# Attention and clustered feed-forward layer on one core: the last quad's threshold by token, TensorE taking any over tokens, two dense tiles moved out of unit 31

## The reference, cut to what matters

```python
x = x + attention(layernorm(x), w_qkv, w_o)     # 32 heads, 8 kv heads, causal, sqrt-distance bias
y = layernorm(x)
dots = softmax(y @ centroids.T / 0.1)           # 64 clusters
hits = dots > 0.01
query_sel = any(hits, axis=clusters)            # one flag per token
cluster_sel = any(hits, axis=tokens)            # one flag per cluster, over all 2048 tokens
row_sel = cluster_sel[assignments]              # one flag per output column
dense = y @ weight.T + bias
x = x + where(query_sel & row_sel, dense, 0)
```

## Time and profile before

| what | us |
|---|---|
| runs: 1267.18, 1268.92, 1269.65; median | 1268.92 |
| the profiled execution's own time | 1267.08 |
| its span, first to last instruction | 1265.4 |
| TensorE busy | 1242.9 (98%) |
| TensorE weight loads | 1050.6 (83%) |
| VectorE busy | 767.6 (61%) |
| ScalarE busy | 751.8 (59%) |
| GpSimd busy | 515.5 (41%) |

### The profile page before, as it was taken

One profiled execution on the slowest core, in us unless ns is written; L12 is line 12 of the kernel. 1 busy time (PEld: TensorE's weight loads), 2 busy tenths in 40 slices (PEclk: granted clock), 3 DMA queues, 4 the chain that ended last, 5 costly groups with the idle time before them and its releaser, 6 DMA issues.

```text
span 1265.4 us, 21888 instructions
## 1 busy us (share of the span) xinstructions
PE 1242.9 (98%) x6166; PEld 1050.6 (83%) x6166; DVE 767.6 (61%) x2160; ACT 751.8 (59%) x2154; POOL 515.5 (41%) x476
## 2 busy tenths in 40 slices
PE   7899999999999999999999999999999999999997
PEld 6688888888888888888888888888888888888876
DVE  8777555555555555565555555655555556667677
ACT  3776566666655666666556666665565666656543
POOL 5322645227342455226442364327362364223223
PEclk9999999999999999999999999999999999999999
DMA  6422334334332343424333344323343343412103
GB/s 195 161 87 88 117 124 157 108 108 141 94 132 89 120 145 124 133 99 133 102 123 107 119 147 124 125 91 128 99 146 116 111 146 116 134 62 99 49 21 133
DMA packets 162377, 147.14 MB, mean 116 GB/s; under 512 B 10032, under 2 KB 123696, under 8 KB 162352
## 3 DMA queue, kind: packets, MB, share of 16 engines
q1 hardware_dynamic: 156528, 128.48, 30.6%
q0 software_dynamic: 5824, 18.36, 4.9%
HBM read 84.67 MB, written 62.13 MB: 116 GB/s over the span
## 4 chain that ended last, share of the span: by engine, by line
PE 87%; DVE 6%; ACT 3%; issue 2%; DMA 1%; POOL 0%; DVEq 0%; SPq 0%; ACTq 0%
PE ps L1206 81%; PE ps L1285 3%; PE ps L1286 1%; ACT prob L678 1%; ACT prob L669 1%; DVE ring_whole L905 1%; DVE stats L826 1%; PE ps L1226 1%; DVE qT_lo L880 1%; DVE rs L851 0%; DVE prob L865 0%; DVE prob L942 0%; DMA acc<-in_L_attn_hidden_states 0%; DVE acc L1127 0%; DVE selected L984 0%
## 5 line engine op out<-in xcount | busy, mean ns | idle before, releaser
L1206 PE MATMUL ps<-xnT,wqkv_hi 128*128 (+1 forms) x1568 | 486.4, 391 | 5.0 <-DVE negmax L942 2.8
L515 POOL TENSOR_TENSOR ring<-ring_whole,pT_hi 128x512 fp32r<-128x512 f32 x189 | 243.7, 1289 | 486.6 <-ACT pT_hi L658 486.3
L1206 PEld LDWEIGHTS ps<-xnT,wqkv_hi 128*128 128x128 f32 x1568 | 292.1, 188 | 66.6 <-issue 5.0
L669 ACT ACTIVATE prob<-prob,negmax 128x128 f32<-128x128 f32 (+1 forms) x512 | 226.8, 445 | 181.9 <-DVE negmax L942 180.9
L1206 PE MATMUL ps<-xnT,wqkv_lo 128*128 (+1 forms) x784 | 305.8, 390 | 0.0
L678 ACT ACTIVATE prob<-prob,rinv 128x128 f32<-128x128 f32 (+1 forms) x512 | 190.3, 445 | 62.5 <-DVE rinv L950 62.5
L1206 PE MATMUL ps<-wo_hi,oT_hi 128*128 128x512 f32 x512 | 201.8, 394 | 0.0
L1206 PE MATMUL ps<-wo_lo,oT_hi 128*128 128x512 f32 x512 | 199.8, 390 | 0.0
L1206 PE MATMUL ps<-wo_hi,oT_lo 128*128 128x512 f32 x512 | 199.3, 389 | 0.0
L1206 PEld LDWEIGHTS ps<-xnT,wqkv_lo 128*128 128x128 f32 x784 | 147.4, 188 | 31.1
L922 DVE TENSOR_TENSOR acc<-ps,acc 128x512 f32 (+1 forms) x128 | 88.5, 691 | 128.1 <-PE ps L1206 127.9
(11 more groups left out here) (125 smaller groups left out, 1717.2 us busy)
## 6 DMA issues: line engine op xcount, KB each, us to landing
turned<-ring_whole SPq DMA_DIRECT2D x189, 256.0 KB, 2.1
ring_whole<-turned SPq DMA_DIRECT2D x189, 256.0 KB, 3.0
turned_v<-vT SPq DMA_DIRECT2D x32, 256.0 KB, 2.0
vT<-turned_v SPq DMA_DIRECT2D x31, 256.0 KB, 2.8
raw<-in_L_attn_w_qkv POOLq DMA_DIRECT2D x28, 256.0 KB, 3.2
raw<-in_L_attn_w_o POOLq DMA_DIRECT2D x28, 256.0 KB, 3.5
raw<-in_L_attn_w_qkv POOLq DMA_DIRECT2D x28, 128.0 KB, 3.5
acc<-in_L_attn_hidden_states SPq DMA_DIRECT2D x3, 1024.0 KB, 8.2
```

Source lines behind the costliest of these rows:

```text
L515: pool.tensor_tensor(ring_slot(c), whole_slot(c), pT_hi[:, c % 2, :].bitcast(F32), ALU.subtract).then_inc(pT_lo_done, 1)
L669: ins = act.activation(s, s, ACT.Exp, bias=negmax[:, n:n + 1], scale=-1.0, accum_out=rowsum[:, n:n + 1])
L1206: ins = pe.matmul(dst, l, r, start=start and m == 0, stop=stop and m == n - 1)
```

## The change

- Quad 1's `dense(1,0)` and `dense(1,1)`, with their `dense_part`, leave unit 31 and head the tail. On VectorE `dense_part(1,0)` stands between `invert_sums` 2 and 3, and `dense_part(1,1)` behind 3. In the tail `apply_v(32, 0)` moves ahead of `dense(1,3)`.
- Quad 3's logits are computed with tokens on the partitions at once (`logits_by_token`): per tile four matmuls of 128 columns (hi part of x with both halves of `cT`) and four of 64 (lo part of x with the hi half), each with its own stationary operand. ScalarE copies the lo half to SBUF (`copy_low`), VectorE adds it onto the hi half in PSUM and takes the maximum (`last_max`), ScalarE writes the exponentials over the logits in PSUM (`last_exps`), and VectorE compares them with sum times threshold in one instruction (`last_cluster_hits`).
- The maximum over quads and tiles (`any_hit`, quad 3's `quad_hits`) is gone: seven small matmuls accumulate the hits of three quads and of quad 3's four tiles.
- The waits for the mask move ahead of `dense(2,2,(2,3))`; the first half of `dense(2,0)` is put before `transpose_logits(2)`, the second half behind it. VectorE does `cluster_bias(2)` before `ln_lo(7)`, `finish(0,4)` directly behind `cluster_sel`, and both `dense_part(2,0)` and `(2,1)` behind that. ScalarE does `scaled_bias(2)` behind the last exponentials.

```diff
...
@@ -339,6 +343,10 @@
         def whole_slot(c):
 
             return ring_whole[:, c % RING, :]
+
+        def last_logits():
+
+            return ps[:, LAST_LOGITS, :].rearrange("p (t s c) -> p t s c", t=TPQ, s=2)
 
         def by_tail(u, c):
 
@@ -694,6 +702,19 @@
                     at = slice(j * CLUSTERS, (j + 1) * CLUSTERS)
                     ins = act.activation(cl_exp[:, at], ps[:, logit_bank(p), at], ACT.Exp,
                                          bias=cl_bias[:, j:j + 1], scale=INV_TEMP, accum_out=cl_sum[:, j:j + 1])
+                ins.then_inc(cl_exp_done, 1)
+
+            def copy_low():
+
+                act.wait_ge(logit_mm, QUADS)
+                act.activation(logitT[:, 0:TPQ * CLUSTERS].rearrange("p (t c) -> p t c", t=TPQ), last_logits()[:, :, 1, :],
+                               ACT.Copy).then_inc(low_copied, 1)
+
+            def last_exps():
+                act.wait_ge(cl_max_done, QUADS)
+                for j in range(TPQ):
+                    e = last_logits()[:, j, 0, :]
+                    ins = act.activation(e, e, ACT.Exp, bias=cl_bias[:, j:j + 1], scale=INV_TEMP, accum_out=cl_sum[:, j:j + 1])
                 ins.then_inc(cl_exp_done, 1)
 
             def scaled_bias(p):
@@ -803,9 +824,9 @@
             for j in range(TPQ):
                 ln_hi(7, j, LAST)
             cluster_exps(2)
-            copy_logits(3)
+            copy_low()
+            last_exps()
             scaled_bias(2)
-            cluster_exps(3)
             scaled_bias(3)
 
 
@@ -974,6 +995,31 @@
                 dve.tensor_reduce(quad_hits[:, bass.ds(p * CLUSTERS, CLUSTERS)],
                                   cl_exp[:].rearrange("p (t c) -> p c t", c=CLUSTERS), AX_X, ALU.max).then_inc(ffn_step, 1)
                 ffn_wait(p, 4)
+                dve.sem_inc(hits_done, 1)
+
+            def last_max():
+
+                dve.wait_ge(low_copied, 1)
+                logits = last_logits()[:, :, 0, :]
+                dve.tensor_tensor(logits, logits, logitT[:, 0:TPQ * CLUSTERS].rearrange("p (t c) -> p t c", t=TPQ),
+                                  ALU.add).then_inc(last_step, 1)
+                dve.wait_ge(last_step, 1)
+                dve.tensor_reduce(cl_nmax[:], logits, AX_X, ALU.max, negate=True).then_inc(last_step, 1)
+                dve.wait_ge(last_step, 2)
+                dve.tensor_scalar(cl_bias[:], cl_nmax[:], INV_TEMP, None, ALU.mult).then_inc(cl_max_done, 1)
+
+            def last_cluster_hits():
+
+                dve.wait_ge(cl_exp_done, QUADS + 1)
+                dve.tensor_scalar(cl_rinv[:], cl_sum[:], THRESHOLD, None, ALU.mult).then_inc(last_step, 1)
+                dve.wait_ge(last_step, 3)
+                hits = last_hits[:].rearrange("p (t c) -> p t c", t=TPQ)
+                dve.tensor_tensor(hits, last_logits()[:, :, 0, :],
+                                  cl_rinv[:].rearrange("p (t a) -> p t a", a=1).broadcast_to([P, TPQ, CLUSTERS]),
+                                  ALU.is_gt).then_inc(last_ready, 1)
+                dve.wait_ge(last_ready, 1)
+                dve.tensor_reduce(selects(QUADS - 1), hits, AX_X, ALU.max).then_inc(last_step, 1)
+                dve.wait_ge(last_step, 4)
                 dve.sem_inc(hits_done, 1)
 
             def dense_part(p, quad, j):
@@ -1037,6 +1083,7 @@
                 if p is not None:
                     cluster_bias(p)
                     cluster_hits(p)
+                if p == 0:
                     dense_part(p, source, 0)
                 if proj:
                     add_bias(u, 2)
@@ -1045,7 +1092,7 @@
                     add_bias(u, 3)
                     if not is_first(u):
                         invert_sums(u, 0)
-                if p is not None:
+                if p == 0:
                     dense_part(p, source, 1)
                 if attn:
                     add_out(u, 2)
@@ -1128,7 +1175,9 @@
                                     selected[:, at].rearrange("p (t n) -> p t n", t=n)).then_inc(final, n)
 
             invert_sums(u - 1, 2)
+            dense_part(1, 1, 0)
             invert_sums(u - 1, 3)
+            dense_part(1, 1, 1)
             oT_lo_part(u, 0)
             tail_pT_lo_part(3)
             dve.wait_ge(added, u * QTILES)
@@ -1164,24 +1213,21 @@
             ln_scale(7)
             for j in range(TPQ):
                 ln_apply(7, j, 3)
+            cluster_bias(2)
             for j in range(TPQ):
                 ln_lo(7, j, LAST)
-            cluster_bias(2)
             cluster_hits(2)
-            cluster_bias(3)
-            dense_part(2, 2, 0)
-            cluster_hits(3)
-
-            dve.tensor_reduce(any_hit[:], quad_hits[:].rearrange("p (q c) -> p c q", c=CLUSTERS), AX_X,
-                              ALU.max).then_inc(any_ready, 1)
+            last_max()
+            last_cluster_hits()
             dve.wait_ge(sel_mm, 1)
             dve.tensor_scalar(cluster_sel[:], ps[0:CLUSTERS, PV[0], 0:P], 0.0, None, ALU.is_gt).then_inc(csel_ready, 1)
-            dense_part(2, 2, 1)
             dve.wait_ge(sel_mm, 2)
             finish(0, 4)
+            dense_part(2, 2, 0)
+            dense_part(2, 2, 1)
+            finish(4, 4)
             dense_part(2, 2, 2)
             dense_part(2, 2, 3)
-            finish(4, 4)
             dense_part(3, 3, 0)
             dve.wait_ge(dense_out, TPQ * QUADS)
             finish(8, 4)
@@ -1296,6 +1342,18 @@
                     for n, x in enumerate(ffn_x(p)):
                         ins = pe.matmul(ps[:, logit_bank(p), :], cT[:, c, :, :], x[:, c, :], start=c == n == 0, stop=c == NC - 1 and n == 1)
                 ins.then_inc(logitT_mm, 1)
+
+            def logits_by_token(p):
+
+                x_hi, x_lo = ffn_x(p)
+                for j in range(TPQ):
+                    pe.wait_ge(ln_lo_done, p * TPQ + TPQ * QUADS + j + 1)
+                    at = slice(j * P, (j + 1) * P)
+                    dst = ps[:, logit_bank(p), at]
+                    for c in range(NC):
+                        pe.matmul(dst, x_hi[:, c, at], cT[:, c, :, :], start=c == 0, stop=False)
+                        ins = pe.matmul(dst[:, 0:CLUSTERS], x_lo[:, c, at], cT[:, c, 0, :], start=False, stop=c == NC - 1)
+                ins.then_inc(logit_mm, 1)
 
             def transpose_logits(p):
                 pe.wait_ge(logitT_copied, p + 1)
@@ -1426,12 +1485,15 @@
 
             u = UNITS
             pe.wait_ge(v_lo_done, u)
+            pe.wait_ge(oT_lo_done, u * QTILES)
+            dense(1, 0)
+            dense(1, 1)
             pe.wait_ge(added, u * QTILES - 1)
             dense(1, 2)
+            pe.wait_ge(dense_out, TPQ + FFN_TAIL)
+            apply_v(u, 0)
             pe.wait_ge(scores_biased, u * SCORE_BANKS)
             dense(1, 3)
-            pe.wait_ge(dense_out, TPQ + FFN_TAIL)
-            apply_v(u, 0)
             pe.wait_ge(cl_exp_done, 3)
             transpose_probs(u, 3)
             apply_v(u, 1)
@@ -1458,27 +1520,31 @@
             project_out(u, 3)
             cluster_logits(2, u)
             pe.wait_ge(added, u * QTILES + 2)
-            dense(2, 0)
+            dense(2, 0, (0, 1))
             transpose_logits(2)
+            dense(2, 0, (2, 3))
             pe.wait_ge(added, u * QTILES + QTILES)
             for j in range(TPQ):
                 ln_transpose(7, j)
+            logits_by_token(3)
             dense(2, 1)
-            cluster_logits(3, None)
             dense(2, 2, (0, 1))
-            transpose_logits(3)
-            dense(2, 2, (2, 3))
-            pe.wait_ge(cl_exp_done, 4)
-            dense(2, 3)
-            dense(3, 0, (0,))
-            pe.wait_ge(any_ready, 1)
-
-            pe.matmul(ps[0:CLUSTERS, PV[0], 0:P], any_hit[:], ones[:], start=True, stop=True).then_inc(sel_mm, 1)
+            pe.wait_ge(hits_done, QUADS - 1)
+            any_hits = ps[0:CLUSTERS, PV[0], 0:P]
+            for p in range(QUADS - 1):
+                pe.matmul(any_hits, quad_hits[:, p * CLUSTERS:(p + 1) * CLUSTERS], ones[:], start=p == 0, stop=False)
+            pe.wait_ge(last_ready, 1)
+            for j in range(TPQ):
+                ins = pe.matmul(any_hits, last_hits[:, j * CLUSTERS:(j + 1) * CLUSTERS], ones[:], start=False, stop=j == TPQ - 1)
+            ins.then_inc(sel_mm, 1)
             pe.wait_ge(csel_ready, 1)
             pe.wait_ge(onehot_ready, 1)
 
             pe.matmul(ps[:, MASK_BANK, :], cluster_sel[:], onehot[:], start=True, stop=True).then_inc(sel_mm, 1)
-            dense(3, 0, (1, 2, 3))
+            dense(2, 2, (2, 3))
+            pe.wait_ge(cl_exp_done, QUADS)
+            dense(2, 3)
+            dense(3, 0)
             dense(3, 1)
             dense(3, 2)
             dense(3, 3)
```

## The result

The changed kernel's median is 1264.09 us (6 runs, 1262.71 to 1264.34), the kernel before has 1268.87 (6 runs): ratio 0.9966, 95% interval 0.9956 to 0.9976. In a second session, on one chip beside the first experiments, it was 1264.38 against 1267.46, ratio 0.9971 (0.996 to 0.9983). Faster, by 0.3%. The profiled execution took 1262.71, the fastest of its six.

The account below looks back on a forecast made before the run. TensorE and VectorE were both taken to press on the end, their last stretch starting from the mask. TensorE's -2.5 and VectorE's -0.45, against a schedule's 3.4, became -3.2: 1265.7 us from median 1268.92, range 1263.4 to 1268.8.

Parts of the forecast that it names:

- The sum: TensorE's terms to the end: -0.9 + 1.2 - 1.3 - 1.5 = -2.5 us, with VectorE adding -0.45.
- Two tiles leave unit 31: Unit 31 and tail start: 2.9 us of waits go, 2.25 come; output projection 0 starts 0.7 to 1.1 earlier, taken -0.9.
- Logits by token: Quad 3's logits on TensorE: 32 small matmuls at 0.11 take 3.5 us, plus 0.3 waiting; net +1.2 us.
- The threshold chain at the old forms' prices: Quad 3's threshold, table load to last compare (1234.0 to 1241.6), priced by old forms; its 2.8 us sum bounded by half and double.
- The hole: TensorE's gap in dense work at the mask: 1.9 us instead of 3.2, giving -1.3.
- The clock: TensorE behind the mask: the 2.4 GHz level holds throughout after the shorter hole, giving -1.5 us.
- The schedule's 3.4: Gain by the schedule at VectorE's end: last dense part and copy finish at 1259.4 against 1262.84, 3.4 us.
- The rounding up from 2.95 to 3.2: Final gain taken as -3.2 us, above the summed terms and 0.2 short of the schedule for semaphores.
- the moved tiles return nothing: Rival: unit 31's new waits equal the old ones; gain -2.3, 1266.6 us; chance 0.09.
- the clock still falls: Rival: TensorE's clock falls behind the 1.9 us hole, paying 1.5 again; gain -1.7, 1267.2 us; chance 0.16.
- small matmuls were not dear: Rival denied here: logits matmuls cost 0.21 to 0.227 each, ending 3.2 to 3.7 later; -0.5, 1268.4 us; chance 0.12.
- the queue was not held: Rival denied here: late threshold chain holds TensorE's queue; at double price, hole 4.7, +1.1, 1270.0 us; chance 0.07.

Follow-up runs that it names:

- the first experiments: Kernel before with moved tiles alone (1266.74 us); changed kernel with those tiles back (1265.68); kernel before with an unused SBUF tensor (1266.96); changed kernel again (1264.38).
- e5: Kernel before plus 18 unused transposes filling TensorE's hole before the any-hit matmul; 1268.30 us, ratio 1.0.
- e1: Kernel before with only dense(1,0) and dense(1,1) moved out of unit 31; 1266.74 us, ratio 0.9989.
- e3: Kernel before with one unused SBUF tensor declared, shifting addresses as in the change; 1266.96 us, ratio 0.9997.
- e6: Changed kernel with quad 3's logits computed the old way and all of dense(2,2) ahead of the mask's waits; 1264.83 us, ratio 0.9976 to before.
- e13: Changed kernel with the any-hit matmuls and mask moved behind dense(2,3), three half tiles later; 1270.48 us, ratio 1.0021 to before.
- e10: Changed kernel with the mask's waits half a tile earlier, all of dense(2,2) behind the mask; 1267.16 us, ratio 0.9989 to before.
- e12: Changed kernel with three matmuls before the cluster_sel wait and dense_part(2,0) before the first masked copy; 1263.74 us, ratio 0.9971 to before.

## Why the prediction was right, point by point

The forecast was 1265.7 us, range 1263.4 to 1268.8; measured 1264.09. By the medians the gain was 4.8 us in the first session and 3.1 in the second against 3.2 forecast. By the trace it is 2.5. The mechanism held and single terms were off; that the median came out 1.6 below the forecast is not the change's doing but chance or what no run here explains.

- **The sum.** By the measure, TensorE's last matmul ends 2.07 us earlier, against -2.5. Term by term it is -0.49 for the moved tiles (-0.9), +1.16 for the logits (+1.2), -1.14 for the hole (-1.3) and -1.58 for the clock (-1.5). VectorE adds 0.4 as said.
- **Two tiles leave unit 31, -0.9:** the one term clearly mis-sized. Its own parts came to 2.9 - 2.25 = 0.65 and were raised to 0.9 for small waits that no bracket shows. Measured, the tail returns 2.6 net (2.45 in the parts) and unit 31 costs 2.0 (1.8). Output projection 0 starts 0.55 earlier by the measure (26.31 behind the mark against 26.86), where 0.7 to 1.1 was forecast, and `cluster_logits(2)` 0.49. `add_bias` 2 did not start at once behind the threshold: VectorE idled 0.33 us there.
- **Logits by token, 0.11 a matmul, 3.5 us:** 3.59. The 0.3 us of waiting for `ln_lo(7)` was 0.36.
- **The threshold chain at the old forms' prices:** from the table load to the last compare 7.79 us (1232.72 to 1240.51) against 7.6 predicted. The addition into PSUM took 0.43, a maximum 0.42, the compare 0.42. That 0.42 was taken from a maximum; the old compares' own 2.25 is in no line of the prediction. An exponential written to PSUM takes 0.28 to 0.29 us, one written to SBUF 0.31 to 0.32, but with the read of the sum behind each both start 0.29 to 0.30 apart; so the advantage that the Trainium skill, page "ScalarE: Activation LUTs", section "Step-by-step: what each stage is for", gives to PSUM shows in the single instruction and is worth nothing here.
- **The hole, 1.9 us:** 2.1. Counted from the mark, TensorE reached it 0.6 later than in the schedule (1240.9 on the old trace) and left it 0.75 later (1242.8).
- **The clock, -1.5 on TensorE:** the size was right, 1.58 in e5, though it was worked out with 45 steps where 45 matmuls have 44. The prediction said VectorE had hidden it before; e5 shows that. No profile with a hole of 2.1 us or less at the mask lost the clock behind it; all three with 3.2 (before, e1, e3) did, and so did 2.9 (e6) and the 3.24 of e13.
- **The schedule's 3.4** was too good by 0.9: dense work came back 0.75 late, of which the moved tiles are 0.4, and the 66 matmuls behind the mask took 15.3 us instead of 15.1. The rounding up from 2.95 to 3.2 was the wrong way.
- **The 1.8 us at the start** was in no term. It is scatter of the profiled execution, and whether such scatter brought the first session's median to 4.8 isn't shown.

Of the rivals, "the moved tiles return nothing" was half true; "the clock still falls" did not happen at the mask, but e10, e12 and e13 show a fall in a place that I had not named; small matmuls were not dear, and the queue was not held. VectorE waited for TensorE before the last part but one (1.24 us), not before both of the last two.

## What to carry to other kernels

When two engines press on the end, price a loss on one of them only after asking whether the other hides it: 1.6 us of clock were free until the copies started earlier. A mask or flag that all of the output waits for is worth moving ahead of work that doesn't need it, but the engine's list must then be filled around each handover, and every bank that the moved work frees must be freed in time. Where executions scatter by more than the effect, measure from the last event that the change cannot touch to the end, in several profiles.

## What the runs showed of the hardware that was not expected

- TensorE's granted clock fell to 0.50 in three of the nine profiles that have the 32 small matmuls (128 and 64 columns, each with its own weight load), in e10, e12 and e13, as these ended, while the engine was busy without a gap (2.00 of 2.00 us in e10's stretches from 1235 to 1239): the dense matmuls behind them lost 1.7 to 1.8 us. Idle holes are not the only thing that costs the clock. The Trainium skill, page "TensorE: Matmul & The Clock Gate", section "What's actually happening", says the clock follows how busy the array was and names only an idle stretch for the fall; these three profiles go beyond it.
- From the threshold's transposes to `dense(2,1)` TensorE's list is the same in all nine, so the fall there goes by the execution and not by the edits. What decides it was not settled. The five profiles without the small matmuls show no fall at that place.
- Four `TENSOR_SCALAR` of 128x64 on VectorE took 2.25 us while GpSimd was adding, and 0.74 while it was idle, in each of the four profiles with the old threshold.
- The time from the first instruction to unit 31 scattered by 3.3 us between profiles. The landing of the first input tiles is part of it (1.0 us between the profiles before and after), and a granted clock below 1.00 between 40 and 60 us in some profiles another (0.9 us in the repeat of the changed kernel).
